# Null-row operations of a second attention moved one to two steps earlier, with GpSimd's prepared sums placed between the first null parts

## What is computed

```python
x = x + attn(cond(x, bias, mask, ...), Wq, bq, Wk, bk, Wv, bv, gamma)
x = x + ffn(cond2(x, ...), w_router, w_block)

def attn(x, ...):                 # 8 heads, dqk = 4, dv = 32
    scores = einsum('bmhd,bnhd->bhmn', q, k) / sqrt(dqk)
    scores = where(scores >= 0, scores, 0.2 * scores)
    beta = softmax(scores, axis=-1)
    return gamma * einsum('bhmn,bnhd->bmhd', beta, v) + x
```

## Time and profile before

| | us |
|---|---|
| median of 3 runs | 393.2 |
| lowest, highest | 392.29, 393.77 |
| the profiled execution | 392.07 |
| its span, first to last instruction | 390.3 |

### The profile page before, as it was taken

How to read it: one execution, slowest core, us unless ns; L and a number is a source line. 1 busy time by engine, 2 the same in 40 slices (tenths; PEclk the granted TensorE clock), 3 DMA queues, 4 the chain that set the end, 5 groups by cost and what they waited for, 6 DMA issues and landing times.

```text
span 390.3 us, 5777 instructions
## 1 busy us (share of the span) xinstructions
PE 308.1 (79%) x1625; PEld 210.9 (54%) x1625; DVE 205.9 (53%) x730; ACT 135.7 (35%) x428; POOL 182.2 (47%) x306
## 2 busy tenths in 40 slices
PE   0399999988998977996384799919999998058890
PEld 0246766646765744543342456517888886035680
DVE  0724554531732445687157455514555554099996
ACT  0246677663011167562120000003555555014440
POOL 1308998862020000128701878751666666166380
PEclk9999999999999675599698599988999999559996
DMA  4879930000029500000100222224555541542006
GB/s 127 252 188 292 301 98 3 2 0 3 0 85 317 126 0 0 3 0 0 29 1 0 94 93 85 91 86 138 159 158 163 152 129 54 180 149 103 0 2 216
DMA packets 36185, 37.84 MB, mean 97 GB/s; under 512 B 5422, under 2 KB 31791, under 8 KB 36146
## 3 DMA queue, kind: packets, MB, share of 16 engines
q1 hardware_dynamic: 31762, 28.90, 25.4%
q0 software_dynamic: 3408, 8.41, 6.2%
q10 hardware_dynamic: 976, 0.08, 0.2%
HBM read 21.74 MB, written 16.55 MB: 98 GB/s over the span
## 4 chain that ended last, share of the span: by engine, by line
PE 23%; POOL 10%; DVE 9%; DMA 4%; issue 3%; ACT 1%; DVEq 0%; POOLq 0%; SPq 0%
PE psU L2490 9%; PE psY L2508 4%; POOL XS L2370 4%; POOL XS L2379 4%; DVE Y L2749 3%; DMA YR<-YS 3%; PE psG L2480 2%; POOL pause L2359 2%; DVE WGU L2783 2%; DVE GT L2762 2%; PE psY L2500 1%; PE psU L2558 1%; PE psG L2414 1%; PE psU L2414 1%; DVE eqj L2765 1%
## 5 line engine op out<-in xcount | busy, mean ns | idle before, releaser
L2387 POOL DMA_INDIRECT YS<-YB,IB x39 | 38.4, 984 | 35.0 <-issue 23.2
L2490 PE MATMUL psU<-WGU,XT 128*128 x156 | 41.2, 388 | 0.1
L2600 ACT COPY XT<-psG 128x256 f32<-128x256 f32 x39 | 14.7, 378 | 64.0 <-PE psG L2480 64.0
L1196 POOL TENSOR_SCALAR UU<-UU,rs 128x257 f32<-128x257 f32 x32 | 29.8, 931 | 0.0
L1361 ACT ACTIVATE UU<-UU,nm 128x129 f32<-128x129 f32 x64 | 28.4, 452 | 0.7 <-DVE nm L1470 0.7
L2490 PEld LDWEIGHTS psU<-WGU,XT 128*128 128x128 f32 x156 | 27.2, 194 | 2.7 <-issue 0.5
L1470 DVE CUSTOM_DVE_ANT_0 UU<-psS,BI 128x129 f32<-128x129 f32 x64 | 19.1, 355 | 16.7 <-PE psS L1249 16.7
L1195 POOL TENSOR_SCALAR UU<-UU,rs 128x129 f32<-128x129 f32 x32 | 19.6, 612 | 16.0 <-DVE rs L1480 15.8
L2370 POOL DMA_INDIRECT XS<-AI,SI x16 | 15.7, 981 | 23.8 <-DVE SI L2689 19.7
L857 POOL TENSOR_TENSOR T<-Vn,wn 128x128 f32<-128x128 f32 x8 | 3.0, 398 | 48.0 <-DVE wn L953 48.0
L2733 DVE TENSOR_SCALAR LK<-psU 128x128 f32<-128x128 f32 x39 | 11.3, 291 | 25.7 <-PE psU L2490 25.6
(11 more groups left out here) (313 smaller groups left out, 733.9 us busy)
## 6 DMA issues: line engine op xcount, KB each, us to landing
XS<-PZ SPq DMA_DIRECT2D x1, 5011.5 KB, 20.1
XB<-XS SPq DMA_DIRECT2D x39, 128.5 KB, 2.1
YR<-YS SPq DMA_DIRECT2D x4, 1024.0 KB, 5.4
BI<-in_bias SPq DMA_DIRECT2D x4, 512.0 KB, 8.0
out_dram<-WGU SPq DMA_DIRECT2D x4, 512.0 KB, 3.0
X<-in_x SPq DMA_DIRECT2D x2, 768.0 KB, 10.3
BI<-in_bias SPq DMA_DIRECT2D x4, 256.0 KB, 7.5
Wo<-in_wo SPq DMA_DIRECT2D x1, 1024.0 KB, 7.4
```

The lines of the kernel that those rows point to most:

```text
L1196: pool.tensor_scalar(U[:, he, W1:WU], U[:, he, W1:WU], rs[:, d, 2 * he + 1:2 * he + 2], None, ALU.mult).then_inc(n_done, 1)
L2387: pool.indirect_dma_start(YS[:, :], bass.IndirectOffsetOnAxis(ap=IB[:, b, n:n + 1], axis=0), YB[i][:, n, :], None, bounds_check=2 * NTOK - ...
L2490: mm = pe.matmul(psU[b % 2][:, n * D:(n + 1) * D], XT[b % 2][:, k, n * P:(n + 1) * P], WGU[:, k, bass.ds(which[b], 1), :].rearrange("p a m ...
```

## The change

The null row's operations move up. TensorE: transposes from s = 2 to 1, product with the values from 3 to 2, product with ones from 5 to 3. ScalarE: RA0 from step 0 to between `relu(0)` and `relu(1)`; the exponentials in step 0 stand before `relu(2)` instead of behind it; P0T from s = 2 to 1. VectorE: UU0 and en0 from step 0 to before `ttr(1)`; the division from s = 1 to 0, M0 from 3 to 2, CB from 5 to 3. GpSimd: `early_part(0)` and `early_part(1)` to behind `null_part(0)` and `null_part(1)`. No instruction is added or dropped.

```diff
                                 mm.then_inc(t_done, 1)
-                        if s == 2:
+                        if s == 1:
                             pe.wait_ge(z_dve, 2)
...
-                        if s == 3:
+                        if s == 2:
                             pe.wait_ge(z_act, 3)
...
-                        if s == 5:
+                        if s == 3:
                             pe.wait_ge(z_dve, 3)
...
                     relu(0)
+                    act.wait_ge(z_pe, 1)
+                    act.activation(RA0[:, :], psZ[0:H2, :], ACT.Relu, scale=-0.8).then_inc(z_act, 1)
                     relu(1)
...
-                        if s + 2 < NSP:
-                            relu(s + 2)
                         if s == 0:
-                            act.wait_ge(z_pe, 1)
-                            act.activation(RA0[:, :], psZ[0:H2, :], ACT.Relu, scale=-0.8).then_inc(z_act, 1)
                             act.wait_ge(z_dve, 1)
...
                             act.activation(en0[:, :], en0[:, :], ACT.Exp).then_inc(z_act, 1)
-                        if s == 2:
+                        if s + 2 < NSP:
+                            relu(s + 2)
+                        if s == 1:
                             act.wait_ge(z_pe, 2)
...
                     null_part(0)
-                    null_part(1)
                     pool.wait_ge(z_dve, 4)
                     pool.wait_ge(s_x, 16 * B)
                     early_part(0)
+                    null_part(1)
+                    early_part(1)
                     null_part(2)
-                    early_part(1)
                     null_part(3)
...
+                    dve.wait_ge(z_act, 1)
+                    for b in range(B):
+                        chain(dve.tensor_tensor_reduce(
+                            out=UU0[:, b * KQ:(b + 1) * KQ], in0=psZ[0:H2, b * KQ:(b + 1) * KQ],
+                            in1=RA0[:, b * KQ:(b + 1) * KQ], scale=-1.0, scalar=NL0[:, 0:1], op0=ALU.add, op1=ALU.min,
+                            accum_out=nm0[:, b:b + 1]))
+                    after()
+                    dve.tensor_tensor(en0[:, :], nm0[:, :], NL0[:, 0:1].broadcast_to([H2, B]), ALU.subtract
+                                      ).then_inc(z_dve, 1)
                     ttr(1)
                     for s in range(NSP + 2):
...
                         if s == 0:
-                            dve.wait_ge(z_act, 1)
...
-                        if s == 1:
                             dve.wait_ge(z_act, 2)
...
-                        if s == 3:
+                        if s == 2:
                             dve.wait_ge(z_pe, 3)
...
-                        if s == 5:
+                        if s == 3:
                             dve.wait_ge(z_pe, 4)
```

## The result

| | before | after |
|---|---|---|
| median of 20 runs, us | 393.01 | 388.05 |
| lowest, highest | 387.44, 393.77 | 385.64, 391.84 |
| profiled execution, its span | 392.07, 390.3 | 387.94, 386.2 |

The ratio after to before is 0.9896, 95% interval 0.9867 to 0.9925: 1.0% faster. The 388.6 predicted is within 0.6 us of the median. Medians here are of all runs, while ratios leave out those more than 1.5% above the fastest of the same kernel, so the two need not agree (3 of e6's 12 runs are left in its ratio, 4 of 6 in e5's and e10's).

The account below looks back on a forecast made before the run. GpSimd was taken to end the block last, 6.2 us behind the others. Terms of -4.15 (its sums), -0.4 (outputs(1)) and -0.1 (transposes) gave -4.6, from the median 393.2 to 388.6; range for 8 in 10, 385.2 to 390.9.

Parts of the forecast that it names:

- term 1: GpSimd: the six sums of early_part(0) move into its idle time before null_part(1), -4.15 us.
- by 1.4 us: End of the block: VectorE's last output, at 184.4, is needed at 185.8, so GpSimd still ends last.
- Early part of the chain: RA0, UU0 and en0 before ttr(1) cost nothing; step 1's transposes start about 148.6 for 149.15, half a microsecond won.
- terms 3 and 4: VectorE: CB leaves step 5, where it stood right before outputs(1), -0.8; weights(1) runs beside GpSimd's sums, +0.4.
- term 4: VectorE: weights(1) slowed beside early_part(0), +0.9 less 0.52 idle before ttr(7), +0.4; bounds 0 and +2.2.
- Term 5: TensorE's steps: full clock returns about 161.5 instead of 164.9, half lost again waiting for exponentials, -0.8; bounds 0 and -3.2.
- term 2: TensorE before step 4's scores: the product with ones, 1.1 us at full speed, moves ahead of them, +0.8.
- rival (a): Clock returns 3.6 us into the long run and holds over the smaller hole; outputs(1) moves -2.1, kernel 385.4; chance 0.20.
- Term 6: Next block: TensorE's hole before the expert stage's transposes shrinks to about 2.7 us, -0.1, with -1.5 as other end.
- The signs: Expected in the trace: early_part(0) within 1 us of 168.8, outputs(1) within 1 us of 176.4, last sum ending 185.5 to 187.5.
- signs of being wrong: CB after 171.7, GpSimd's last sum waiting for VectorE, step 2's transposes waiting for exponentials, or half clock after 170.
- Rival (c): Full clock does not come back at 164.9; at half to the end the kernel takes 401, slower; chance 0.05.

Follow-up runs that it names:

- e6: Kernel before with only TensorE's product with P0T moved from step 3 to step 2; median 394.34, ratio 0.9952.
- e5: Changed kernel plus 3 unread 256-column matmuls at the end of TensorE's part of the block; median 386.81, ratio 0.9845 to the kernel before.
- e10: e8 with the unread matmuls of steps 0 to 2 rearranged: 2 and 2 before scores, 1, 3 and 1 before transposes; median 380.35, ratio 0.9746.
- e1: Kernel before with GpSimd's new order alone, the null row's chain left in place; median 392.92, ratio 1.0033.
- e2: Changed kernel with GpSimd's old order, so only the null row's chain moved; median 391.17, ratio 0.9988 to the kernel before.
- e7: e5 plus 1, 2, 3 and 1 unread matmuls in TensorE's holes of steps 5 to 8; median 384.83, ratio 0.9832 to the kernel before.
- e8: e7 plus 2 and 3 unread matmuls ahead of the scores in steps 0 and 1; median 383.46, ratio 0.9808 to the kernel before.
- e4: The changed kernel unchanged, run and profiled once more; median 385.87, ratio 0.9843 to the kernel before, profiled execution 391.08.
- e11: e8 unchanged, run once more; median 383.44, ratio 0.9843 to the kernel before.

## Why the prediction was right, and where not

- **The bound and term 1 (-4.15)** held. GpSimd ends the block in both kernels, and the sums fill the hole before `null_part(1)`. With the clock held it is 3.8: 9.41 became 9.82, mostly since `null_part(3)` waits 0.31 for `weights(3)`, which I had not looked at. e1 and e2 show that both halves are needed, which the prediction used but did not say.
- **The claim that GpSimd stays last "by 1.4 us"** was too wide. After, its last sum starts 0.7 us after VectorE's last output, and it had to wait 1.35 for `outputs(2)`, because the clock fell at 178.9: in e7, e8 and e10, where it did not, that wait is gone. The prediction read from the trace before that the clock outlives holes shorter than 1.5 us. It overlooked that the clock fell at 141.0 in that same trace, right behind a hole of 1.70, and in the changed kernel it fell behind holes of 1.42 and 1.46 in the steps. That part of the reading failed.
- **Early part of the chain, terms 3 and 4.** The transposes of step 1 start at 148.59 for 149.15, the half microsecond forecast (0.2 of it is there before the block's changed part: the scores of step 1 are at 137.80 for 137.98). CB left step 5. `weights(1)` beside the sums took 1.62 us (170.03 to 171.65) for 0.86; forecast 1.75. Another 0.27 went into the small operation ahead of it (line 987, 0.43 us for 0.16), and the idle time before `ttr(7)` took up all but 0.17 of the other 0.76, so that term 4 measured +0.44 for +0.4. All four operations held for a whole sum each, as the prediction put the lock of the Trainium skill's page "SBUF — State Buffer" ("Who interferes with whom"), would have made it 3.6; the trace again shows some holding (0.65 us for an operation of 0.17), a good quarter of that price. The reciprocal kept its 0.20 us, and the same section leaves an operation with one SBUF input, as it is, out of the lock.
- **Term 5 (-0.8)** is the one mis-sized. In the profiled execution the clock came back 3 us sooner than I took, and `outputs(1)` moved by -2.45, not -0.4. The scores of step 4 show it: they start at 164.99 for 167.08, so terms 2 and 5 together are -2.1 and were forecast to cancel. With term 2 as counted (+0.8) term 5 was about -2.9, near its bound of -3.2 and past the 2.5 that rival (a) let through: TensorE waited only 0.8 us for exponentials there (0.47 and 0.33 in step 3), not for half of what the clock gave. Its reason failed too: e6 has the long run and no early return, e1 has the return without it. The size fits neither profiled execution: in e4's the sum behind `outputs(1)` comes 1.05 us later than before, in the other 2.44 sooner.
- **Term 6 (-0.1)**: the clock fell in the smaller hole at 185.8. From the first transpose to the start of their last copy it took 5.1 us for 5.8, so -0.7. It rose again after nothing but transposes, against the sentence that the prediction cites from the page "TensorE: Matmul & The Clock Gate".
- **Not in the sum**: the expert loop's slow start, +1.0 in this pair.
- **The signs.** Of those that the prediction named, these came: `early_part(0)` ended before `null_part(1)`, the last sum ended at 186.1, TensorE idled 2.33 us before the transposes, `weights(1)` took 1.62, the clock was at full before 164.9. Two did not: `early_part(0)` started at 167.47 and `outputs(1)` at 174.39, 1.3 and 2.0 us sooner than forecast. And of its signs of being wrong one came: the clock was at half after 170, from 178.9 to 182.4. The time came out near in spite of it.

That the sum came out near is luck in good part, because the parts missed cancel: term 5 by -2.1 and term 6 by -0.6, against +1.7 for GpSimd's two waits and +1.0 in the expert loop. Some 0.5 more went in small pieces behind the block: the two profiled spans differ by 4.1. What the prediction had right is the mechanism on GpSimd and its price; what it had no account of is that the clock's moments differ from one execution to the next, by more than the whole gain. Rival (a) named the clock's early return, which came, and assumed that it would hold, which it did not. Rival (c), the half clock late in the steps, happened in a milder form in the heap at 391.

**Open:** what decides whether the clock falls at 162 in one execution and not in another of the same kernel. Open too is why the changed kernel is in its better heaps more often. The unread matmuls show that the hole ahead of the next block matters. For the holes in steps 0 to 2 there is one profiled execution of e10, with e8 and e11 against any simple rule; it does show that scores 4 rows deep do not prevent full speed.

## What to carry to other kernels

Work that an engine could do in its waits is worth moving only together with what it waits for: here the prepared sums and the chain that feeds them gave 1.0% to 1.6% together and nothing measurable one by one. Compare orders at equal clock, or in rows that do not wait for TensorE: several heaps of times with the mean granted clock beside each say that one execution's trace is one case of several, and a median then also tells how often each heap came. Where the critical engine is another, filling TensorE's holes with matmuls that nobody reads can add to the reordering (e10 380.35 against 392.15 for the kernel before beside it, where the reordering alone gave 1.0% to 1.6%), as long as they end before the engine that bounds the block. e10's gain is 1.6% to 3.5% by its interval, from six runs.

## What was not expected of the hardware

- One kernel, the same inputs, and 6 us between its runs (385.3 to 391.8), going with a mean clock of 0.905 or 0.892.
- The same kernel, profiled twice with the same hole of 0.81 us before 139.8, held the clock to 144.2 (e8) and lost it at 140.9 (e11). With more holes filled it was at full for 68 us (e10, one execution).
- A hole ahead of the transposes of 2.1 to 8.3 us cost the clock in six executions of six, one of 0.3 to 1.6 us in none of seven.
